# Taking the mean and variance of half of the tiles on ScalarE, in an eight-core attention and FFN layer

## The reference

```python
xn = layernorm(x)                                  # (x - mean) / sqrt(var + 1e-5), no weights
logp = log_softmax(xn); p = exp(logp)
cross = einsum('bid,bjd->bij', p, logp)
kl = sum(p * logp, -1)[:, :, None] - cross
attn = softmax(-kl)                                # over j: the first term of kl drops out
out = einsum('bij,bjd->bid', attn, xn)
gate = xn @ (w_gate/127).T ; up = xn @ (w_up/127).T
ffn = (silu(gate) * up) @ (w_down/127).T
x = x + out + ffn
```

## Time and profile before

| | us |
|---|---|
| median of 4 runs | 845.29 (844.84 to 846.5) |
| profiled execution, its own time | 845.5 |
| span of its slowest core, core 0, first to last instruction | 843.9 |
| spans of the eight cores | 840.4 to 843.9 |
| PE busy / VectorE busy / ScalarE busy | 757.8 (90%) / 268.8 (32%) / 200.5 (24%) |

### The profile page before, as it was taken

One profiled execution on the slowest core, in us unless ns is written; L12 is line 12 of the kernel. 1 busy time (PEld: TensorE's weight loads), 2 busy tenths in 40 slices (PEclk: granted clock), 3 DMA queues, 4 the chain that ended last, 5 costly groups with the idle time before them and its releaser, 6 DMA issues.

```text
span 843.9 us, 9386 instructions; the slowest of 8 cores (840.4 to 843.9 us)
## 1 busy us (share of the span) xinstructions
PE 757.8 (90%) x3840; PEld 355.6 (42%) x3840; DVE 268.8 (32%) x308; ACT 200.5 (24%) x236; POOL 12.6 (1%) x25
## 2 busy tenths in 40 slices
PE   0235799999999999999999999999999999999997
PEld 0134344444444444444444444444444444444443
DVE  4987121102002001114511451145114511451146
ACT  2577750340430510221022102210221022102210
POOL 5000000000000000000000000000000000000000
PEclk9965799999999999999999999999999999999999
DMA  7999999996000033522310231024102310000027
GB/s 224 240 109 108 111 108 110 113 103 74 1 1 1 1 73 73 102 52 57 76 19 1 56 65 30 1 56 74 21 1 56 73 22 1 0 2 0 1 100 299
DMA packets 82889, 55.17 MB, mean 65 GB/s; under 512 B 78160, under 2 KB 78160, under 8 KB 82272
## 3 DMA queue, kind: packets, MB, share of 16 engines
q0 software_dynamic: 2976, 27.30, 23.7%
q1 hardware_dynamic: 79872, 27.28, 13.6%
HBM read 46.17 MB, written 27.26 MB: 87 GB/s over the span
## 4 chain that ended last, share of the span: by engine, by line
PE 87%; DVE 5%; ACT 4%; issue 2%; DMA 2%; POOL 0%; DVEq 0%; ACTq 0%; POOLq 0%
PE ps L184 13%; PE ps L585 10%; PE ps L597 10%; PE ps L600 10%; PE ps L588 10%; PE ps L657 10%; PE ps L660 10%; PE ps L428 7%; PE ps L430 7%; DMA x_sb<-x 2%; DVE scr L271 1%; PE ps_bf L317 1%; DVE st_bn L221 1%; ACT scr L614 1%; DVE st_bn L223 1%
## 5 line engine op out<-in xcount | busy, mean ns | idle before, releaser
L657 PE MATMUL ps<-arena 128*128 128x512 bf16 x384 | 145.5, 379 | 8.7 <-ACT scr L614 4.6
L628 DVE TENSOR_TENSOR arena<-scr,ps 128x1024 bf16<-128x1024 f32 x48 | 58.6, 1221 | 281.8 <-ACT scr L614 281.8
L585 PE MATMUL ps<-xnT,arena 128*128 128x512 bf16 x384 | 145.6, 379 | 1.8 <-DVE x_sb L443 1.8
L597 PE MATMUL ps<-xnT,arena 128*128 128x512 bf16 x384 | 145.6, 379 | 0.0
L600 PE MATMUL ps<-xnT,arena 128*128 128x512 bf16 x384 | 145.5, 379 | 0.0
L588 PE MATMUL ps<-xnT,arena 128*128 128x512 bf16 x384 | 145.5, 379 | 0.0
L660 PE MATMUL ps<-arena 128*128 128x512 bf16 x384 | 145.5, 379 | 0.0
L669 DVE SCALAR_TENSOR_TENSOR x_sb<-ps,x_sb 128x1024 f32<-128x1024 f32 x96 | 117.5, 1224 | 50.8 <-PE ps L660 50.7
L184 PE MATMUL ps<-arena,xnT 128*128 128x512 bf16 x512 | 114.7, 387 | 3.6 <-ACT arena L204 3.6
L614 ACT ACT_TABLE_LOAD x24 | 30.8, 1283 | 319.6 <-PE ps L600 319.6
L428 PE MATMUL ps<-arena 128*128 128x512 bf16 x256 | 96.3, 376 | 5.8 <-ACT arena L204 4.5
(11 more groups left out here) (46 smaller groups left out, 387.4 us busy)
## 6 DMA issues: line engine op xcount, KB each, us to landing
x_sb<-x POOLq DMA_DIRECT2D x8, 1024.0 KB, 17.7
o<-x_sb SPq DMA_DIRECT2D x16, 512.0 KB, 2.7
wg_bf<-wg POOLq DMA_DIRECT2D x4, 1536.0 KB, 82.3
wu_bf<-wu POOLq DMA_DIRECT2D x4, 1536.0 KB, 96.6
wd_bf<-wd POOLq DMA_DIRECT2D x4, 1536.0 KB, 174.3
arena<-wg_bf SPq DMA_TRANSPOSE x48, 3.0
arena<-wu_bf SPq DMA_TRANSPOSE x48, 3.0
arena<-wd_bf SPq DMA_TRANSPOSE x24, 4.2
```

What stands on the lines that cost most here:

```text
L585: te.matmul(base[:, 0:512], lg, xnT_sl(dc, th * 1024, 512), start=st_, stop=sp_)
L597: te.matmul(base[:, 1024:1536], lu, xnT_sl(dc, th * 1024, 512), start=st_, stop=sp_)
L628: E[("hact", idx)] = mark(v.tensor_tensor(out=hact_sl(hcb * 2048 + th * 1024, 1024), in0=scr32[:, th * 1024:(th + 1) * 1024], in1=base[:, ...
L657: te.matmul(ps03[:, q5 * 1024: q5 * 1024 + 512], lh, wdT_sl(b2, hcb * 1024, 512), start=st_, stop=sp_)
```

## The change

Pass 1 of tiles 8 to 15 moves from VectorE to ScalarE. On ScalarE one block is put between pass 2 of pairs 0, 1 and pass 2 of pairs 2, 3. For each of the eight tiles it waits for the load, runs `Square` over 128 x 1024 with its sum accumulated into `st_sq`, waits for that, runs `Copy` over the same tile with its sum into `st_sum`, and the next tile waits for that Copy. The element-wise output of both is thrown away into `ps47[:, 0:1024]`. VectorE gets a small conversion, `emit_conv`, once for tiles 8 to 11 (at k = 0) and once for tiles 12 to 15 (at k = 2): four operations on 128 x 4 that form mean and E[x^2] - mean^2 in `st_mv2`. The `bn_stats` and `bn_aggr` of tiles 8 to 15 leave the loop, and pass 2 of pairs 4, 5 moves from k = 1 to k = 0, that of pairs 6, 7 from k = 3 to k = 2.

```diff
--- before.py
+++ after.py
@@ -62,6 +62,8 @@
         st_s = sb("st_s", [128, NT], F32)
         st_rs = sb("st_rs", [128, 2], F32)
         st_lns = sb("st_lns", [128, NT], F32)
+        st_sum = sb("st_sum", [128, NT], F32)
+        st_sq = sb("st_sq", [128, NT], F32)
         st_neglse = sb("st_neglse", [128, NT], F32)
         recd = sb("recd", [128, 2], F32)
         s_lx = ctx.enter_context(nc.semaphore("lx"))
@@ -244,8 +246,48 @@
 
             for t in range(8):
                 emit_pass1(t)
-            for pr in range(4):
-                emit_pass2(pr)
+            emit_pass2(0)
+            emit_pass2(1)
+
+            @block.scalar
+            def _(a):
+                trash = ps47[:, 0:1024]
+                ev = None
+                for t in range(8, 16):
+                    wt(a, E[("xq8", t // 2)])
+                    wt(a, ev)
+                    e1 = mark(a.activation(trash, xs(t), AF.Square,
+                                           accum_out=st_sq[:, t:t + 1]), "ac")
+                    wt(a, e1)
+                    E[("p1a", t)] = ev = mark(
+                        a.activation(trash, xs(t), AF.Copy,
+                                     accum_out=st_sum[:, t:t + 1]), "ac")
+
+            emit_pass2(2)
+            emit_pass2(3)
+
+            def emit_conv(g0):
+                @block.vector
+                def _(v, g0=g0):
+                    wt(v, E[("p1a", g0 + 3)])
+                    sl = st_mv2[:, 2 * g0: 2 * g0 + 8].rearrange(
+                        "p (t two) -> p t two", two=2)
+                    mark(v.tensor_scalar(
+                        out=sl[:, :, 0:1], in0=st_sum[:, g0:g0 + 4],
+                        scalar1=1.0 / D, scalar2=None, op0=ALU.mult), "dv")
+                    ee = mark(v.tensor_scalar(
+                        out=sl[:, :, 1:2], in0=st_sq[:, g0:g0 + 4],
+                        scalar1=1.0 / D, scalar2=None, op0=ALU.mult), "dv")
+                    wt(v, ee)
+                    ee = mark(v.tensor_tensor(
+                        out=st_sq[:, g0:g0 + 4], in0=sl[:, :, 0:1],
+                        in1=sl[:, :, 0:1], op=ALU.mult), "dv")
+                    wt(v, ee)
+                    ee = mark(v.tensor_tensor(
+                        out=sl[:, :, 1:2], in0=sl[:, :, 1:2],
+                        in1=st_sq[:, g0:g0 + 4], op=ALU.subtract), "dv")
+                    for t in range(g0, g0 + 4):
+                        E[("mv", t)] = ee
 
             def emit_xnTe(eng, t):
                 qp = t % 2
@@ -365,15 +407,14 @@
                         emit_xnTe(a, t0 - 1)
 
                 if k < NT // 2 - 1:
-                    if k < 4:
-                        emit_pass1(8 + 2 * k)
-                        emit_pass1(9 + 2 * k)
-                        if k == 1:
-                            emit_pass2(4)
-                            emit_pass2(5)
-                        if k == 3:
-                            emit_pass2(6)
-                            emit_pass2(7)
+                    if k == 0:
+                        emit_conv(8)
+                        emit_pass2(4)
+                        emit_pass2(5)
+                    if k == 2:
+                        emit_conv(12)
+                        emit_pass2(6)
+                        emit_pass2(7)
                     emit_dve_pre(t0 + 2)
                     emit_dve_pre(t1 + 2)
                 if k < 6:
```

## The result

The changed kernel takes 861.99 us (median of 7 runs, 860.88 to 862.77) against 845.42 (10 runs, 844.59 to 846.5): a ratio of 1.0194, 95% interval 1.0183 to 1.0205, so 16.4 us slower, with 15.5 to 17.3 as the interval. 861.0 was forecast. Every kernel here has executions in which the cores of a die show a lower granted clock and the time is some per cent longer; all times and ratios are of the others alone. The profiled execution took 861.99 us; its slowest core is core 6 with a span of 860.5, and the others lie between 856.5 and 859.6.

The account below looks back on a forecast made before the run. VectorE was taken to bound four of the start's steps, a ScalarE and PE loop the last two, with ScalarE in every step's chain. 845.5 + 20.9 of late start - 5.5 given back = 860.9, forecast 861, range 856 to 867.5.

Parts of the forecast that it names:

- Where it starts: ScalarE's added block waits only for the fifth load of x, tiles 8 and 9, landing at 23.7 us.
- The sixteen activations: Square and Copy of eight tiles on ScalarE, 1.22 us each, 19.5 us in all; ends 16.6 and 24.
- What is queued behind: Two pass 2 and the first Exps follow the block on ScalarE; first Exps at 48.5, late by 20.9 us.
- What the steps give back: Steps 0 to 5, with pass 1 of eight tiles off VectorE, take 45.9 us against 51.4: 5.5 us back.
- Conversions: Two on VectorE, about 1 us each, cost nothing: one in the wait for first Exps, one in step 2.
- The sum: Whole kernel: 845.5 + 20.9 - 5.5 = 860.9 us, that is + 15.4, given as 861.
- the clock term: TensorE's clock at M1 may be lower or higher after longer idling; 1.5 us allowed either side, nothing in the sum.
- The steps do not speed up: Rival: something else holds the loop's steps at their old pace, so only the delay stands: 866.4 us; 6 in 100.
- Hidden by the casts: Rival: the FFN waits for the weight casts, so a late M1 does not matter: 845.5 us; 3 in 100.
- The relief wins: Rival: ScalarE's added work fits its idle time before 27.57, so the steps' 5.5 us gain stands: 840 us; 2 in 100.
- A table load for each change of function: Rival: Square and Copy share no table set on ScalarE; fifteen more loads add 19.3 us: 880; 4 in 100.
- delay and relief: The sum's two terms: first Exps on ScalarE late by 20.9 us, and steps 0 to 5 giving back 5.5 us.

Follow-up runs that it names:

- the two targets: Changed kernel with Square and Copy writing to different halves of the PSUM scratch, each waiting only for the one two before: 857.88 us, ratio 1.0161.
- the relief by itself: Changed kernel without ScalarE's sixteen activations and the conversions, mean and variance of tiles 8 to 15 set to 1: 838.87 us, ratio 0.9932.
- the kernel with the cost only: Kernel before with the sixteen activations added in the same place on ScalarE, their sums unused: 862.63 us, ratio 1.0213.

## Why the prediction was right

The forecast was right in sign and size, 861.0 against 861.99 and inside 856 to 867.5, and in its mechanism, a late start less what the steps give back; only the source of the second term was in part another. Step by step:

- **Where it starts.** 23.7 for the landing of the fifth load; the block began at 23.39 on the slowest core and between 22.64 and 24.10 over all eight.
- **The sixteen activations.** 1.22 each and 19.5 in all; measured 1.24 and 19.76. The wait was the right thing to price, as the two targets show: the low end of 1.04 is what they take without it. The Trainium skill (page "ScalarE: Activation LUTs", section "What ACT_TABLE_LOAD costs") has back-to-back activations overlap by 93 ns, by which they would start 0.95 apart. With an accumulator this was not seen: 1.04 even without waits. In the copies without one it is there, 0.91 apart at a length of 1.01.
- **What is queued behind.** First Exps at 48.5, late by 20.9; measured 48.26 and 20.7.
- **What the steps give back.** 7.35, 7.34, 9.15 and three of 7.34, 45.9 in all; measured 45.91, and the relief by itself gives the same 45.95. But the prediction put all 5.5 down to VectorE's relief, and the kernel with the cost only, where VectorE keeps its pass 1, has 48.04: 3.4 of the 5.5 come with the late start alone, and 2.1 are the relief's. The claim that pass 2 of pairs 6 and 7 comes out of its cover holds: step 2 is 9.26.
- **Conversions.** At nothing; they were 0.7 each, not 1. The first lies in VectorE's wait for the Exps. The second has no wait ahead of it, but VectorE is not the bound of that step: it waits 0.29 us later in it and 1.56 us ahead of the next step's first post.
- **What failed in size.** The sum was 1.1 us short on the changed kernel's own 861.99 less 845.5 and 15.4. On the profiles' slowest cores 15.2 are there at M1 and 1.4 come behind it. Of these, 1.2 are the length of M1's second group, 32 matmuls in 9.96 us against 8.75: the clock term, put at nothing with 1.5 allowed, and told below. The mean of the eight cores divides it otherwise. M1's second group begins 16.0 later and 0.8 come behind, because the landings of the sum were read on core 0, the latest of its eight. So the missing 1.1 lie in part in the start and in part in the clock, and no run separates them.
- **The rivals.** "The steps do not speed up" fell (45.95 without the block). "Hidden by the casts" fell: the casts ended as before, and the end moved by the 16.4. Its margin was also reckoned the wrong way: a later M1 adds to the 92.7, so the casts would have had to end more than 92.7 us later to hide any of it, and 108 to hide it all, not 77. "The relief wins" would have needed activations of 0.26 and is what the relief alone shows, at 838.9. "A table load for each change of function" fell: one load a block. The reckoning of delay and relief as two terms was right only because the step lengths were worked out for the late start; as separate effects they are + 18.0 and - 5.7, which add to 12.3 and not to 16.4.
- **A reading.** PE's last slice stands at 7 tenths and not at 9; nothing in the sum rests on it.

## What to carry to other kernels

Before work is moved from the bound engine to an idle-looking one, look whether the idle one lies in the same chain: its gaps inside a step (here 2.0 us once VectorE is relieved) are what it can take for nothing, and what runs over the gap is paid, wherever the piece stands. The gain of relieving an engine ends at the next loop (12.3 us taken off, 5.7 back), so move only as much as makes both equal: one tile in two, a piece of 2.5 us each step, with pass 2 merged to fit behind it, turned the same idea from 16.4 us slower to 5.3 us faster. Two effects measured apart need not add, when one of them opens a wait that hides the other.

## What the runs showed of the hardware

The time from M1's second group to the end is not the same on all cores: from the start of that group to the start of VectorE's last operation it is 738.2 us on core 5 of the changed kernel, 739.9 on core 7 and 741.1 on core 6. The first ten us of that stretch on the three cores, in this order; the columns are the length, busy time and count of PE, PEld, DVE, ACT and POOL, PE's granted clock, DMA share and GB/s:

```profile
113.93:123.93 10.00, 10.00 (x59) 5.04 (x60) 2.36 (x6) 4.82 (x7) 0.00 (x0) 1.00 0.96 105
```

```profile
114.85:124.85 10.00, 10.00 (x51) 4.70 (x52) 0.87 (x3) 4.71 (x7) 0.00 (x0) 0.83 0.97 105
```

```profile
115.10:125.10 10.00, 10.00 (x36) 4.02 (x37) 0.17 (x1) 3.56 (x5) 0.00 (x0) 0.71 1.04 108
```

The granted clock is 1.00, 0.83 and 0.71 of full speed, and PE does 59, 51 and 36 matmuls in the same 10 us (some records can be missing). PE had stood idle for 3.5, 3.6 and 4.7 us ahead of the group, in the same order, and on core 6 the group begins with 4 us at 0.50, the 1.2 GHz level. Before, core 1 had 738.0 and core 0 739.8. PE's timelines of these two, at the same group:

```profile
98.04 7.07 PE L184 MATMUL ps<-arena,xnT 128*128 128x512 bf16 x32 [3.16 <-ACT arena L204]
```

```profile
99.92 8.75 PE L184 MATMUL ps<-arena,xnT 128*128 128x512 bf16 x32 [3.61 <-ACT arena L204]
```

On cores 5, 7 and 6 of the changed kernel the same 32 matmuls take 7.07, 8.75 and 9.96 us, so this one group holds the whole difference of 1.7 to 2.9 us. Over the eighty cores of the ten profiles the order is without exception: the twenty groups of 7.07 us have the shortest idle times ahead of them (3.12 to 3.51), the seven of 9.96 to 10.02 us the longest (4.60 to 4.66), and the other 53 take 8.35 to 8.75. The idle time itself hangs on what came before it. The second group begins 12.27 or 12.28 us after the first on each of these five cores, so where the first group ran faster (7.61 us on core 6, 8.75 on core 5) the wait behind it was longer. Which of the two decides, the wait or the work ahead of it, and why the first groups differ, no run here shows.

The other thing not expected: ScalarE loads its table once at the head of each separately emitted block, even where the block before ended in the same functions (L238 at 44.45 and again at 46.35, both Ln and Exp), and not between Exp, Copy, Square and Ln inside one. A load takes 1.28 us and the activation starts 0.01 behind it.
